# The clip of the attention moved to GpSimd, one bias matmul in the output pass, and expert weights waited for piece by piece

## The reference

```
x = x + layernorm(rs * (attention(layernorm(x), context, mask) @ Wo.T + bo)) * gamma + beta
x = x + mixture_of_experts(layernorm(x))
```

## Time and profile before

| | us |
|---|---|
| median of 3 runs | 6835.75 (6833.43 to 6835.9) |
| the profiled execution | 6831.15 |
| its span, from first to last instruction | 6829.2 |

### The profile page before, as it was taken

The page is one execution under the profiler, slowest core; times in us unless marked ns, Lnnn a source line. Parts: engine busy times, 40 slices in busy tenths (PEclk is TensorE's granted clock), DMA queues, the critical chain, the costliest instruction groups (busy, mean ns, idle before and its releaser), DMA issues.

```text
span 6829.2 us, 104167 instructions
## 1 busy us (share of the span) xinstructions
PE 6695.8 (98%) x34594; PEld 5941.0 (87%) x34595; DVE 3294.1 (48%) x4252; ACT 3004.1 (44%) x3636; POOL 1120.7 (16%) x1013
## 2 busy tenths in 40 slices
PE   9999999999999999799999999999999999999998
PEld 7888887887888777699999999999999999999998
DVE  4443325999999798632443333322422323333333
ACT  3222225888888545333444344422422333333333
POOL 1000000000000255411111111111111111111111
PEclk9999999999999999899999999999999999999999
DMA  8863555555555666465776667654644556556665
GB/s 259 228 197 144 156 138 145 130 129 126 128 128 133 181 165 169 136 154 121 189 200 166 157 163 185 162 123 105 184 105 105 136 128 164 147 139 159 159 148 149
DMA packets 692631, 1047.87 MB, mean 153 GB/s; under 512 B 259953, under 2 KB 490097, under 8 KB 692530
## 3 DMA queue, kind: packets, MB, share of 16 engines
q0 software_dynamic: 109792, 368.12, 24.8%
q1 hardware_dynamic: 426352, 381.24, 21.7%
q10 hardware_dynamic: 156386, 297.29, 12.6%
HBM read 724.14 MB, written 322.31 MB: 153 GB/s over the span
## 4 chain that ended last, share of the span: by engine, by line
PE 53%; DMA 2%; issue 1%; ACT 1%; DVE 1%; ACTq 0%; SPq 0%; POOLq 0%; DVEq 0%
PE moe_ps_gate L1332 5%; PE moe_ps_gate L1333 5%; PE moe_ps_gate L1334 5%; PE moe_ps_up L1334 5%; PE moe_ps_y L1321 5%; PE moe_ps_up L1332 5%; PE moe_ps_up L1333 5%; PE moe_ps_y L1319 5%; PE moe_ps_y L1320 5%; PE moe_ps_xT L1309 3%; DMA out<-moe_y,moe_rec_s 1%; PE moe_ps_hT L1340 1%; DMA moe_rec_s<-table 1%; ACT moe_y L1371 0%; DVE moe_gu_lo L1426 0%
## 5 line engine op out<-in xcount | busy, mean ns | idle before, releaser
L1332 PE MATMUL moe_ps_gate<-moe_gu_hi,moe_xT_hi 128*128 128x384 f32 x2288 | 793.3, 347 | 25.4 <-DVE moe_gu_lo L1426 20.9
L1436 DVE TENSOR_TENSOR moe_hidden<-moe_silu,moe_ps_up 128x384 f32<-128x384 f32 x286 | 158.5, 554 | 1305.1 <-PE moe_ps_up L1334 1016.6
L1333 PE MATMUL moe_ps_gate<-moe_gu_lo,moe_xT_hi 128*128 128x384 f32 x2288 | 768.9, 336 | 0.0
L1334 PE MATMUL moe_ps_gate<-moe_gu_hi,moe_xT_lo 128*128 128x384 f32 x2288 | 768.5, 336 | 0.0
L1334 PE MATMUL moe_ps_up<-moe_gu_hi,moe_xT_lo 128*128 128x384 f32 x2288 | 765.1, 334 | 0.0
L1332 PE MATMUL moe_ps_up<-moe_gu_hi,moe_xT_hi 128*128 128x384 f32 x2288 | 764.2, 334 | 0.0
L1333 PE MATMUL moe_ps_up<-moe_gu_lo,moe_xT_hi 128*128 128x384 f32 x2288 | 764.2, 334 | 0.0
L1371 ACT ACTIVATE moe_y<-moe_ps_y,moe_rec_s 128x1024 f32<-128x1024 f32 x287 | 320.7, 1117 | 906.5 <-PE moe_ps_y L1321 494.7
L1319 PE MATMUL moe_ps_y<-moe_d_hi,moe_hT_hi 128*128 128x512 f32 x1722 | 700.4, 407 | 1.9 <-DVE moe_hT_lo L1441 1.9
L1289 POOL DMA_INDIRECT out<-moe_y,moe_rec_s x287 | 458.6, 1598 | 1443.1 <-ACT moe_y L1371 1370.1
L1321 PE MATMUL moe_ps_y<-moe_d_hi,moe_hT_lo 128*128 128x512 f32 x1722 | 677.3, 393 | 0.0
(11 more groups left out here) (202 smaller groups left out, 14172.5 us busy)
## 6 DMA issues: line engine op xcount, KB each, us to landing
first_raw<-in_w_gate ACTq DMA_DIRECT2D x63, 1536.0 KB, 7.0
first_raw<-in_w_up ACTq DMA_DIRECT2D x63, 1536.0 KB
moe_raw_d<-in_w_down ACTq DMA_DIRECT2D x63, 1536.0 KB
proj_a_raw<-in_ctxT POOLq DMA_DIRECT2D x64, 512.0 KB, 5.0
kst<-proj_o SPq DMA_DIRECT2D x256, 128.0 KB, 2.8
vst<-proj_o SPq DMA_DIRECT2D x64, 512.0 KB, 2.6
qst<-proj_o SPq DMA_DIRECT2D x256, 128.0 KB, 2.2
att_kt<-kst SPq DMA_DIRECT2D x64, 512.0 KB, 3.6
```

Of the source, the lines that this page charges most:

```text
L1332: nc.tensor.matmul(o[:, 0:I], xT_hi[:, c], gu_hi[:, b, k, c], start=(c == 0), stop=False)
L1333: nc.tensor.matmul(o[:, 0:I], xT_hi[:, c], gu_lo[:, b, k, c], start=False, stop=False)
L1334: last = nc.tensor.matmul(o[:, 0:I], xT_lo[:, c], gu_hi[:, b, k, c], start=False, stop=(c == C - 1))
```

## The change

Three things are changed.

1. In the attention, `clip` moves from DVE's queue to POOL's, one `tensor_scalar` for each of the 512 units as before, with the minimum first and the maximum second. POOL's DMAs of the sums move into the same queue, to the last pair of each batch. A `sem_inc` on `pool_passed` stands between the second wait and the instruction.
2. In the output pass, the high and low rows of the bias stand in rows 0 and 32 of a tile of 128 rows that is otherwise zero, and one matmul that contracts over all 128 rows adds both.
3. In the experts, PE waits for the split weights piece by piece, all 8 pieces are split ahead of `output` and of the high part of `hT`, the token's weight is multiplied in DVE's `hidden` (from a record `rec_w` that SP loads in addition) rather than in ACT's `output`, `output` waits for the addition before it rather than for `rec_s`, and POOL's `add` waits for `rec_s`. ACT's loop over the experts has its first two peeled.

```diff
+                def clip(n, u, bt):
+                    pool.wait_ge(exp_done, n + 1)
+                    if not (isinstance(n, int) and n < 2):
+                        pool.wait_ge(lo_done, n - 1)
+                    pool.sem_inc(pool_passed, 1)
+                    nc.gpsimd.tensor_scalar(p32[:, u % 2], e32[:, u % 2], upper[:, bt, u % C:u % C + 1], math.exp(-CLIP),
+                                            ALU.min, ALU.max).then_inc(clip_done, 1)
...
+                        if bt and i == NH // 2 - 1 and u == 1:
+                            load_sums(bt - 1)
+                        if bt and i == NH // 2 - 1 and u == 9:
+                            store_inverses(bt - 1)
...
-                def clip(n, u, bt):
-                    dve.wait_ge(exp_done, n + 1)
-                    if not (isinstance(n, int) and n < 2):
-                        dve.wait_ge(lo_done, n - 1)
-                    nc.vector.tensor_scalar(p32[:, u % 2], e32[:, u % 2], math.exp(-CLIP), upper[:, bt, u % C:u % C + 1],
-                                            ALU.max, ALU.min).then_inc(clip_done, 1)
...
-                    nc.tensor.matmul(o[:, b, cols], ones_row[:], bo_hi[:, cols], start=False, stop=False)
-                    nc.tensor.matmul(o[:, b, cols], ones_row[:], bo_lo[:, cols], start=False, stop=True).then_inc(gemm_done, 1)
+                    nc.tensor.matmul(o[:, b, cols], ones_rows[:], bo_rows[:, cols], start=False, stop=True).then_inc(gemm_done, 1)
...
+                    sp.wait_ge(hidden_done, t + 2)
+                    sp.sem_inc(sp_passed, 1)
+                    record(rec_w, t + 1, rec_w_in)
...
+                    pool.wait_ge(rec_s_in, 16 * (t + 2))
+                    pool.sem_inc(pool_passed, 1)
                     pool.wait_ge(y_done, t + 3)
...
-                        if e is not None:
-                            pe.wait_ge(w_lo_done, PIECES * e + (k + 1) * (C // 2))
                         for c in range(C):
+                            if e is not None and c % 2 == 0:
+                                pe.wait_ge(w_lo_done, PIECES * e + k * (C // 2) + c // 2 + 1)
...
-                def output(t):
+                def output(t, is_first=False):
                     act.wait_ge(down_done, t + 2)
-                    act.wait_ge(rec_s_in, 16 * (t + 2))
-                    nc.scalar.activation(y[:], y_ps[:], ACT.Copy, scale=rec_s[:, 1:2]).then_inc(y_done, 1)
+                    if not is_first:
+                        act.wait_ge(added, 16 * (t + 1))
+                    nc.scalar.copy(y[:], y_ps[:]).then_inc(y_done, 1)
...
                     if e is not None:
-                        split(e, b, 0, EARLY)
-                    output(t - 1)
+                        split(e, b, 0, GU)
+                    output(t - 1, is_first)
                     act.wait_ge(hT_done, t + 2)
                     nc.scalar.copy(hT_hi[:], hT_ps).then_inc(hT_hi_done, 1)
-                    if e is not None:
-                        split(e, b, EARLY, GU)
...
-                    nc.vector.tensor_tensor(hidden[:], silu[:], up_ps[:, 0:I], ALU.mult).then_inc(hidden_done, 1)
+                    dve.wait_ge(rec_w_in, 16 * (t + 1))
+                    nc.vector.scalar_tensor_tensor(out=hidden[:], in0=silu[:], scalar=rec_w[:, 1:2], in1=up_ps[:, 0:I],
+                                                   op0=ALU.mult, op1=ALU.mult).then_inc(hidden_done, 1)
                     tokens_low(t + 1)
                     if e is not None:
-                        split(e, b, 0, EARLY)
+                        split(e, b, 0, GU)
                     dve.wait_ge(hT_hi_done, t + 1)
                     nc.vector.tensor_tensor(hT_lo[:], hT_ps, f32(hT_hi[:]), ALU.subtract).then_inc(hT_lo_done, 1)
```

More of the change, by code:

```diff
@@ L532, in _ @@
                     sp.wait_ge(stored[b], 32 * NPAIR)
[L534 to L542, removed]
             def pairs(eng, body):
@@ L556, in pairs, with _, load_sums, store_inverses @@
                     body(bt * n + n - 1, bt, bt + 1 if bt < B - 1 else None, False, n - 1)
+            @block.gpsimd
+            def _(pool):
+                def clip(n, u, bt):
[5 more added lines that the diff above has]
+                                            ALU.min, ALU.max).then_inc(clip_done, 1)
+                def load_sums(bt):
+                    for b in range(2):
+                        pool.wait_ge(stored[b], 32 * (bt + 1) * (NH // 2))
+                    pool.dma_start(sums_t[:], sums[bt * C:(bt + 1) * C].rearrange("k h n -> (k h) n")).then_inc(sums_in, 16)
+                def store_inverses(bt):
+                    pool.wait_ge(inverted, bt + 1)
+                    pool.dma_start(rsums[bt * C:(bt + 1) * C].rearrange("k h n -> (k h) n"), rsums_t[:]).then_inc(inverses_stored, 16)
+                pool.wait_ge(upper_ready, 1)
+                clip(0, 0, 0)
+                def body(pair, bt, next_bt, first, i=None):
+                    for u in range(U):
+                        n = pair * U + u
+                        if u + 1 < U:
+                            clip(n + 1, u + 1, bt)
+                        elif next_bt is not None:
+                            clip(n + 1, 0, next_bt)
+                        if bt and i == NH // 2 - 1 and u == 1:
+                            load_sums(bt - 1)
+                        if bt and i == NH // 2 - 1 and u == 9:
+                            store_inverses(bt - 1)
+                pairs(pool, body)
+                pool.wait_ge(inverses_stored, 16 * (B - 1))
             @block.tensor
@@ L842, in _ @@
             def _(pool):
+                nc.gpsimd.memset(f32(bo_rows[:]), 0.0).then_inc(bo_zeroed, 1)
                 nc.gpsimd.memset(ident[:], 0.0).then_inc(set_up, 1)
@@ L953, in _ @@
                 act.wait_ge(small_in, 32)
-                nc.scalar.copy(bo_hi[:], bo_row[:]).then_inc(bo_ready, 1)
+                act.wait_ge(bo_zeroed, 1)
+                nc.scalar.copy(bo_rows[HI_ROW], bo_row[:]).then_inc(bo_ready, 1)
                 act.wait_ge(rs_ready, 2)
@@ L1184, in experts_pass @@
         y = s.sb("y", [P, H])
-        ident, rec_g, rec_s = s.sb("ident", [P, P]), s.sb("rec_g", [P, 2]), s.sb("rec_s", [P, 2])
+        ident, rec_g, rec_w, rec_s = s.sb("ident", [P, P]), s.sb("rec_g", [P, 2]), s.sb("rec_w", [P, 2]), s.sb("rec_s", [P, 2])
         gate_ps, up_ps, hT_ps = s.ps("gate", [P, HALF]), s.ps("up", [P, HALF]), s.ps("hT", [P, HALF // P, P])[:, 0:CI]
@@ L1235, in _ @@
                 sp.dma_start(rec_g[:], table[REGION:REGION + P, :]).then_inc(rec_g_in, 16)
+                sp.dma_start(rec_w[:], table[REGION:REGION + P, :]).then_inc(rec_w_in, 16)
                 for loaded in raw_in[:2]:
@@ L1409, in expert @@
                     if has_next:
-                        expert_tiles(act, e, lambda t: tile(t, e + 1, 1 - b, has_second), tile)
+                        expert_tiles(act, e, lambda t: tile(t, e + 1, 1 - b, has_second, isinstance(e, int) and e == 0), tile)
                         split(e + 1, 1 - b, GU, PIECES)
@@ L1415, in expert @@
                         expert_tiles(act, e, tile, tile)
-                experts(act, expert)
+                experts(act, expert, peel=True)
                 last_tile = act.value_load(dir_sb[0:1, last_at:last_at + 1], min_val=E - 1, max_val=MAX_TILES - 2)
```

27 lines of the change are left out of this document (11 added, 16 removed).

## The result

The changed kernel takes 6847.94 us (median of 15 runs, 6844.86 to 6851.04); the kernel before, on the same chip, takes 6832.2 (15 runs, 6826.46 to 6836.05). The ratio is 1.0022, interval 1.0014 to 1.003: slower by 0.22%, 16 us. Forecast was slower by 229 us. The profiled execution took 6847.55 us, with a span of 6845.9 (before: 6829.2).

What follows compares the result with a forecast made beforehand. PE was taken to set the pace everywhere. From the profiled 6831 us, +260 (clip and `low` in turns), -19 (bias) and -12 (experts) gave 7060 us; own range 6860 to 7220, stretched to 6775 to 7220 to hold 8 in 10.

Steps and rivals of the forecast that it cites:

- take turns: Attention: POOL's clip and DVE's `low`, with two SBUF inputs, exclude each other for the whole instruction; +260 us.
- The rival without turns: Attention: clip and `low` interleave, the 21 us of late units go, 6779 us in all; chance 0.20.
- the price of the pair: Attention: `low` plus clip cost 2.83 us a unit against PE's 2.27; 512 units make 1449 us, +260.
- the affine select's 0.20 us over the memset: Attention, clip's price: all fixed gives 1.04 us for 1024 elements, all per element 1.67; 1.4 taken.
- The second rival, turns that fit: Attention: with a 1.04 us clip and free hand-overs the pair takes 2.26 us, 6800 in all; chance 0.08.
- Each operation a pass: Attention: the clip takes twice 1.6 us, +1182, 7980 us in all; chance 0.10 together with the falling clock.
- the clock falls: Attention: granted clock drops to 1.2 GHz, 4.5 us a unit, 7930 us; chance 0.10 together with the two-pass clip.
- The bias: Output pass: one full-height matmul takes 34 us from PE, of which -19 us was forecast, bounds -34 and 0.
- its own limit: Output pass: DVE's waits for the product, 21 us, are all the bias can give before DVE sets the pace.
- The experts: Experts: piecewise waits shorten six PE stalls for split weights; -12 us, at most 33 saved, other bound +10.
- 7 for certain: Experts: in six one-tile experts the next silu comes 1.1 us sooner, 7 us in all.
- The new record load: Experts: `rec_w`, issued behind `hidden` and needed a tile (13.7 us) later, is hidden, as a slow record took 6.7 us.

Runs made afterwards that it cites:

- e3: Changed kernel with the attention's `low` replaced by two bn_stats of 512 columns, one SBUF input each: 6787.04 us, attention 1172.0.
- e7: Changed kernel with each clip as two instructions of 512 columns: 6888.79 us, attention 1271.1.
- e11: Changed kernel with the clip's operations on GpSimd in the order of before, maximum with the constant first: 7516.44 us, attention 1899.3.
- e9: Kernel before with only the output pass of after, one full-height bias matmul for two of one row: 6819.29 us, ratio 0.9979.
- e8: Changed kernel with the clip in place in four buffers and `beta` added on 64 of 1024 columns only: 6831.55 us, output pass 509.3.
- e10: Kernel before with only the experts of after: 6821.4 us, ratio 0.998.
- e6: Changed kernel with the clip's maximum left out, one minimum for each element: 7072.64 us, attention 1453.6.

## Why the prediction was wrong, and where it was right

**The direction and the mechanism were right.** `low` and the clip take turns, at one cycle for each unit, and that cycle and no longer PE sets the pace. The rival without turns is out: `low` would have stayed at 1.22 us, and it went to 1.88. e3 and the copies of the heads show the cause that was named, the two SBUF inputs.

That POOL holds up DVE as well, which no row of before showed, is now in the rows: 1.88 us instead of 1.22 for a `low` that starts in a clip. The rule of the Trainium skill that was cited for it ("SBUF — State Buffer", "Who interferes with whom") agrees with these rows in that either one can hold up the other. That the clip does so for its whole instruction does not come out: `low` is held for the first 0.97 us of it, whether it lasts 1.12, 2.83 or 3.69 us (last section).

**The step that failed is the price of the pair**, "1.22 (`low`) + 1.40 (clip) + 0.16 (POOL's start behind its wait) + about 0.05 (hand-over to DVE) = 2.83 us". Two of its terms were off, 0.45 us together:

- *The clip, 1.12 instead of 1.40: 0.28 us, 143 us in 512 units.* It lay within the bounds of 1.04 to 1.67, near the lower one. I read the affine select's 0.20 us over the memset as in part a price for each element. For the clip what it has over a memset is fixed: 1024 columns take 1.119 us and 512 take 0.687 (e7), so 0.84 ns for each element, exactly the memset's slope, and 0.25 fixed. "Two operations are done on each element" was no reason to go up from the middle; in this form the second operation costs nothing that shows.
- *The hand-overs: 0.17 us, 87 us in 512 units.* I put `low` whole behind the clip. It is issued during the clip, is held only for the clip's first 0.97 us, and ends 1.07 us after the clip's end, 0.15 less than a whole `low`. POOL's start was 0.19 instead of 0.16, and the estimate of 0.05 for DVE's start falls away: -0.15 - 0.05 + 0.03 = -0.17. This is why the time fell below even the forecast's lower end of 2.47 us for a unit, though the clip lay within its bounds.

Put in, they make 1449 - 143 - 87 = 1219 us for the attention; measured were 1232.3. The 13 us left are of two kinds. The four batches took 304.8, 309.9, 305.4 and, up to the start of the last unit, 303.2 us: 1223.3 for 511 units, 7 us over 511 x 2.38. These are longer units, which the forecast took to be within the rounding, and 5 of the 7 us lie in the second batch, the one with the weights' subtractions (309.9 against 128 x 2.38 = 304.6). The other 9.0 us of the pass are the last unit's 2.4 and 6.6 us of ends, where the forecast set 512 bare units against a whole pass.

With the clip's price alone the forecast would have been 6917. The range of 6775 to 7220 holds the measured 6848 by luck: it was stretched down to reach the rival without turns, which is out, and the forecast's own range began at 6860. The second rival, turns that fit, said that it is decided at a clip of about 1.05 us less its start. The measured 1.12 lies on the slow side of that, by so little that the loss is 44 us and not 260. It had a chance of 0.08 and was 48 us off, the forecast 212. The Trainium skill's "roughly line-rate" ("GPSIMD Engine Reference", "Engine selection") gave an estimate of 0.85 us. For the form used that was off by 0.27, about as much as my 1.40; for the two other forms it is off by a factor of three and four.

**Each operation a pass, the clock falls.** The form of the change shows no second pass. Yet a price that no row of before excluded did exist, 3.69 us in e11, and putting the constant second is all that kept this kernel from it. The granted clock stayed at 1.00 in the attention though PE had a gap in nearly every unit, and also in e11 with its units of 3.68 us:

```profile
1105.00:3000.00 1895.00, 1318.20 (x5114) 923.67 (x5113) 717.83 (x610) 1018.73 (x1056) 1890.29 (x518) 1.00 0.33 83
```

**The bias, forecast -19, measured -16.7 (e9: -15.5): right**, by its own limit. From the product to what follows the bias are 0.47 us instead of 0.98, 0.51 saved on PE where 0.52 was worked out, and as foreseen less than the whole of it was to be had. A tile went from 15.72 us to 15.25 in the mean. The 24.6 us that DVE waited for the product are 3.5 in two places. PE waits 21.2 us for the normalised rows instead, of which 7.1 is one wait at the pass's end that was there before (7.4). That DVE is the bound in its place is argued from this; e8 didn't settle it.

**The experts, forecast -12, measured -9.5 (e10: -13.4): right.** The waits for split weights were broken up as foreseen, 20.9 us to 1.9, and the waits behind what ACT and DVE do grew: for `hidden` from 0.5 us to 7.8, for the tokens' low part from 4.5 to 7.6. "7 for certain" held. The new record load was judged hidden with a tile to spare, and that step was wrong. It isn't issued right behind `hidden`: on SP it stands behind the load of `rec_s`, which waits for an addition. In the longest of DVE's seven waits, `hidden` had ended at 3082.48, the load was issued at 3091.49 and `hidden` began at 3097.74, 6.57 us late. PE stood 0.75 us behind that one (0.16 for `hidden`, 0.59 for the tokens' low part behind it on DVE) and not at all behind the six others. So it cost little here, but there was no tile of room.

## What to carry to other kernels

Two instructions that exclude each other cost their sum only where they meet. Before moving work to GpSimd beside a VectorE instruction with two SBUF inputs, give it buffers enough that it starts by its own input and not by the end of that instruction: here the same move cost 44 us with two buffers and gained 22 with four. And price a GpSimd instruction in its exact form, operands and order included; when only other operations are in the trace, let a row of another length decide what is fixed and what is per element before taking a middle (here the memset's slope on the affine select's 0.29 us gave 1.04, and 1.12 was measured). That can't tell the form's own price: no row of before showed that other forms would take 2.83 or 3.69.

## What the runs showed of the hardware

- GpSimd's `tensor_scalar` on 128x1024 fp32 in SBUF: minimum with a value for each partition and then maximum with a constant 1.12 us; that minimum alone 2.83; maximum with the constant first and the minimum second 3.69. Why the shorter instruction takes 2.5 times as long is open.
- A clip holds up a DVE instruction with two SBUF inputs for its first 0.96 to 0.99 us, however long it lasts itself. In the changed kernel, with clips of 1.12 us, 459 `low` start 0.2 to 0.9 us into a clip. They last 1.32 to 1.96 us, and each ends 0.96 to 0.99 us plus a whole `low` of 1.225 after the clip's start. In e6 and in e11, with clips of 2.83 and 3.69 us, the six `low` that start 0.5 us into a clip last 1.67 to 1.70 us and end at the same distance; the other 505 start 1.1 us or more into a clip and take their 1.23 us, but for two of e11 with 1.30 and 1.31. So the medians of 1.226 there don't mean that the turns are gone: `low` comes when the hold is over. (A start on POOL is rough in the profile, but this distance is the same beside all three forms.) Two `low` of e6, the first held and the second not, with the starts of their clips (the second POOL line is two clips in a row):

```profile
2179.09 2.85 POOL L556 TENSOR_SCALAR att_p<-att_e,att_upper 128x1024 f32<-128x1024 f32 x1
2181.91 5.65 POOL L556 TENSOR_SCALAR att_p<-att_e,att_upper 128x1024 f32<-128x1024 f32 x2
...
2179.62 1.68 DVE L667 TENSOR_TENSOR att_p_lo<-att_p,att_p_hi 128x1024 fp32r<-128x1024 f32 x1 [1.58 <-ACT att_p_hi L643]
2183.05 1.23 DVE L667 TENSOR_TENSOR att_p_lo<-att_p,att_p_hi 128x1024 fp32r<-128x1024 f32 x1 [0.62 <-ACT att_p_hi L643]
```

  The weights' subtractions of e6 (0.42 us alone) agree: the 16 that start 0.4 to 0.6 us into a clip take 0.79 to 0.95 us and end 1.38 to 1.40 us into it, and the 16 that start 2.3 us into one take 0.42. One instruction of e11 stands apart. Of its eight subtractions from `att_w_rest` one took 1817 ns instead of 469:

```profile
L693 DVE TENSOR_TENSOR ahead_wo_lo<-att_w_rest,ahead_wo_hi x8: 417/469/1817, 1948.8 to 2052.4; 128x256 fp32r<-128x256 f32 x8
...
2008.41 1.82 DVE L693 TENSOR_TENSOR ahead_wo_lo<-att_w_rest,ahead_wo_hi 128x256 fp32r<-128x256 f32 x1
...
2005.14 11.06 POOL L556 TENSOR_SCALAR att_p<-att_e,att_upper 128x1024 f32<-128x1024 f32 x3
```

  The second of these three clips starts at 2008.83. The subtraction ends 1.40 us into it, as the held ones of e6 do, although it began 0.42 us ahead of it. Why it came second is open.
- A statistic of 512 columns with a single SBUF input (e3) and a copy of 1024 columns from PSUM to SBUF ran beside the clip at 0.69 and 1.21 us, and the clip of e3 stayed at 1.12.
